# Routing logits as extra columns of two projections, and the choice of experts on raw logits

## What is computed

```python
x = x + retention(layernorm(x) @ Wq, layernorm(x) @ Wk, layernorm(x) @ Wv) @ Wo
# retention, per chunk and head: attn = (q k^T) * D;  o = attn v + (q * decay_q) S
#                                S = decay_s * S + (k * decay_k)^T v
t = layernorm(x)
probs = softmax(t @ Wg)                       # 8 experts
top_w, top_i = top_k(probs, 2); top_w /= sum(top_w) + 1e-8
x = x + sum over the chosen e of top_w[e] * (relu(t @ W1[e]) ** 2 @ W2[e])     # W1: 128x256, W2: 256x128
```

## Time and profile before

| what | value |
|---|---|
| median of 3 runs | 287.58 us (287.05 to 288.04) |
| the profiled execution's own time | 287.56 us |
| its span, first to last instruction | 285.8 us |
| busy share of the span: PE, DVE, POOL, ACT | 95%, 77%, 72%, 64% |
| DMA: moved, mean rate | 26.80 MB, 94 GB/s |
| granted clock of PE | 0.999 |
| one loop pass in the middle | 32.58 us |

### The profile page before, as it was taken

One profiled execution on the slowest core, in us unless ns is written; L12 is line 12 of the kernel. 1 busy time (PEld: TensorE's weight loads), 2 busy tenths in 40 slices (PEclk: granted clock), 3 DMA queues, 4 the chain that ended last, 5 costly groups with the idle time before them and its releaser, 6 DMA issues.

```text
span 285.8 us, 8944 instructions
## 1 busy us (share of the span) xinstructions
PE 272.0 (95%) x3662; PEld 214.0 (75%) x3662; DVE 219.2 (77%) x569; ACT 182.7 (64%) x265; POOL 205.3 (72%) x165
## 2 busy tenths in 40 slices
PE   7979859799999999999999999999999999999995
PEld 6566538568887788777887788777887788878883
DVE  3749848996769965996769965896859768998783
ACT  2354569466873697556964687556965567686861
POOL 2114888878969698669968699579968668566452
PEclk9999999999999999999999999999999999999999
DMA  7429043213250251304450250203420252043201
GB/s 233 128 60 304 7 189 100 84 31 124 76 148 2 78 186 48 103 5 136 126 147 2 79 175 15 71 5 108 153 76 2 77 158 90 17 141 119 76 0 73
DMA packets 13577, 26.80 MB, mean 94 GB/s; under 512 B 1120, under 2 KB 6624, under 8 KB 13536
## 3 DMA queue, kind: packets, MB, share of 16 engines
q1 hardware_dynamic: 13536, 26.23, 28.5%
HBM read 24.00 MB, written 2.23 MB: 92 GB/s over the span
## 4 chain that ended last, share of the span: by engine, by line
PE 56%; POOL 17%; issue 15%; DVE 5%; DMA 2%; ACT 2%; POOLq 1%; DVEq 0%
POOL act_lo L1067 14%; PE h_ps L338 7%; PE y_ps L353 6%; PE h_ps L340 6%; PE h_ps L339 6%; PE y_ps L359 6%; PE y_ps L354 6%; PE bank L485 3%; POOL rstd L1021 2%; PE bank L507 2%; PE bank L418 2%; PE bank L497 2%; DMA scale<-scratch 1%; PE bank L450 1%; PE y_ps L317 1%
## 5 line engine op out<-in xcount | busy, mean ns | idle before, releaser
L1067 POOL TENSOR_TENSOR act_lo<-act_f,act_hi 128x512 fp32r<-128x512 f32 x112 | 145.6, 1324 | 46.0 <-ACT act_f L955 45.9
L765 DVE SCALAR_TENSOR_TENSOR act_s<-h_ps,scale 128x1024 f32<-128x1024 f32 x64 | 77.9, 1218 | 29.6 <-PE h_ps L340 13.5
L950 ACT ACTIVATE act_hi<-act_s 128x1024 fp32r<-128x1024 f32 x64 | 67.8, 1059 | 29.7 <-DVE act_s L765 29.5
L955 ACT ACTIVATE act_f<-act_s 128x1024 f32<-128x1024 f32 x64 | 66.8, 1044 | 0.0
L338 PE MATMUL h_ps<-x_hi,w_lo 128*128 128x512 f32 x128 | 53.9, 421 | 1.7 <-DVE attn L658 1.7
L353 PE MATMUL y_ps<-act_hi,w_lo 128*128 128x512 f32 x128 | 53.8, 421 | 0.0
L340 PE MATMUL h_ps<-x_hi,w_hi 128*128 128x512 f32 x128 | 50.6, 395 | 0.0
L339 PE MATMUL h_ps<-x_lo,w_hi 128*128 128x512 f32 x128 | 50.4, 394 | 0.0
L354 PE MATMUL y_ps<-act_hi,w_hi 128*128 128x512 f32 x128 | 50.2, 392 | 0.0
L359 PE MATMUL y_ps<-act_lo,w_hi 128*128 128x512 f32 x128 | 40.4, 396 | 0.1
L1021 POOL TENSOR_TENSOR rstd<-variance,minus_half 128x4 f32<-128x4 f32 x16 | 18.4, 1152 | 19.5 <-DVE variance L622 19.4
(11 more groups left out here) (123 smaller groups left out, 387.8 us busy)
## 6 DMA issues: line engine op xcount, KB each, us to landing
scale<-scratch SPq DMA_DIRECT2D x32, 512.0 KB, 4.0
x_t_in<-x_tr SPq DMA_DIRECT2D x8, 256.0 KB, 4.9
x_all<-x SPq DMA_DIRECT2D x8, 256.0 KB, 4.8
out<-out_sb SPq DMA_DIRECT2D x8, 256.0 KB, 4.1
scale<-w SPq DMA_DIRECT2D x1, 768.0 KB, 4.7
cst<-constants SPq DMA_DIRECT2D x1, 417.0 KB, 4.8
cst<-constants SPq DMA_DIRECT2D x1, 256.0 KB, 2.8
scale<-w SPq DMA_DIRECT2D x1, 256.0 KB, 5.6
```

Source lines behind the costliest of these rows:

```text
L765: nc.vector.scalar_tensor_tensor(out=act_s[:, u % 2], in0=h_ps[:, u % 2], scalar=0.0, in1=scale[:, f % 2, e].unsqueeze(1).to_broadcast([P, ...
L950: nc.scalar.activation(act_hi[:, u % 4], act_s[:, u % 2], ACT.Square).then_inc(act_hi_ready, 1)
L955: nc.scalar.activation(act_f[:, u % 2], act_s[:, u % 2], ACT.Square).then_inc(act_f_ready, 1)
L1067: nc.gpsimd.tensor_tensor(act_lo[:, u % 4, n], act_f[:, u % 2, n], act_hi[:, u % 4, n].bitcast(F32), ALU.subtract).then_inc(pool_low_ready, 1)
```

## The change

The routing logits no longer have a stage of their own. Since x2 = x + rstd * (o Wo), the raw logits x2 @ (centred Wg) are x @ Wg' + rstd * (o @ (Wo Wg')). The first term comes as 8 more columns of the value projection, the second as 8 more of the output projection, whose weights are made once on the chip (`route_outputs`). ACT's `copy_v` copies the first 8 columns for each group next to x (the rows of x_all are 136 wide now), and `add_attention` adds the second with the same instructions that make x2. The two best are found on these raw logits (`rank_experts`, `mark_chosen`), the shift is applied to the sorted values, now from SBUF (`shift_logits`), ACT makes the eight exponentials and two of half the argument, POOL takes the inverse square root of the denominator only (4 values per partition), and DVE multiplies.

With wider groups four of them no longer fit one PSUM bank: the fourth goes to another bank. `project_out` uses bank2 for it, so `project_q(a)` has to wait for x2 and is split from `project_k(a)`. The orders change: on PE slot 1 k, 3 q, 4 transposes of k, 5 value projection; in the start `transpose_roots(0)` stands ahead of `w1_product(0, 0)` and the outputs; on DVE the key is decayed before the query, and the choice is split; on POOL the lower parts of W1 come after the roots.

```diff
-        x_all = sb("x_all", [P, X_RING, GROUPS, P])
+        x_all = sb("x_all", [P, X_RING, GROUPS, WIDE])
+        def v_place(s, g):
+            if g == GROUPS - 1:
+                return ((y_ps[:], h_bank[3])[s] if s < 2 else bank1[:])[:, 0:WIDE]
+            return ((bank1[:], h_bank[2])[s] if s < 2 else bank2[:])[:, WIDE * g:WIDE * (g + 1)]
+
+        def out_place(g):
+            return bank2[:, 0:WIDE] if g == GROUPS - 1 else bank1[:, WIDE * g:WIDE * (g + 1)]
...
+            def route_outputs():
+                pe.wait_ge(second_loaded, DMA)
+                pe.wait_ge(v_z_ready, 1)
+                pe.matmul(y_ps[:, 0:EXPERTS], cst[:, C_WO_T:C_WO_T + P], w_g, start=True, stop=True).then_inc(wog_done, 1)
...
+            def project_q(s):
...
+                else:
+                    pe.wait_ge(x2_ready, s)
+                project(s, 0, q_bank(s), q_done)
...
             def project_v(s):
...
                     pe.wait_ge(q_m_ready, s + 1)
                     pe.wait_ge(q_d_ready, s + 1)
+                    pe.wait_ge(x_hi_ready, s)
...
-                    last = pe.matmul(v_bank(s)[:, P * g:P * (g + 1)], x_t_in[:, s % XT_RING, P * g:P * (g + 1)],
-                                     w_center[:, 2], start=True, stop=True)
+                    last = pe.matmul(v_place(s, g), x_t_in[:, s % XT_RING, P * g:P * (g + 1)], w_vg, start=True, stop=True)
...
-            def route(s):
-                pe.wait_ge(x_sum_ready, s + 1)
...
                     if n == 1:
-                        project_qk(a)
+                        project_k(a)
                     if n == 3:
+                        project_q(a)
+                    if n == 4:
                         transpose_k(a)
-                    if n == 4:
+                    if n == 5:
                         project_v(a)
...
             center_piece(2)
             center_piece(3)
+            center_piece(4)
+            transpose_roots(0)
             w1_product(0, 0)
-            center_piece(4)
             outputs_within(1, (0, 1))
-            transpose_roots(0)
             w1_product(0, 1)
...
+            def rank_experts(s):
+                raw = x_all[:, s % X_RING, :, P:WIDE]
+                dve.wait_ge(x2_ready, s + 1)
+                for g in range(GROUPS):
+                    last = nc.vector.max(best[:, g], raw[:, g])
+                last.then_inc(rank_step, 1)
...
                 for g in range(GROUPS):
-                    last = nc.vector.tensor_scalar(logits[:, g], l_ps[:, g], top[:, g:g + 1],
+                    last = nc.vector.tensor_scalar(shifted[:, g], best[:, g], best[:, g, 0:1],
                                                    rstd[:, 1, s % STAT_RING, g:g + 1], ALU.subtract, ALU.mult)
...
+            def weigh(s):
...
                 dve.wait_ge(expd_ready, s + 1)
+                nc.vector.tensor_reduce(total[:], expd[:], AX_X, ALU.add).then_inc(weigh_step, 1)
...
+                nc.vector.scalar_tensor_tensor(out=denom[:, 0], in0=total[:], scalar=TOP_EPS, in1=expd[:, :, 0],
+                                               op0=ALU.mult, op1=ALU.add).then_inc(weigh_step, 1)
...
-                if a < TILES:
-                    decay_q(a)
                 scale_h(f, 1)
                 low(u)
                 if a < TILES:
                     decay_k(a)
+                    decay_q(a)
                 scale_h(f, 2)
                 low(u + 1)
                 if p < TILES:
+                    rank_experts(p)
                     shift_logits(p)
                 scale_h(f, 3)
                 low(u + 2)
                 if p < TILES:
-                    choose(p)
+                    mark_chosen(p)
+                    weigh(p)
                 if a < TILES:
                     decay_scores(a, decay_order(a)[0:1])
                 scale_h(f, 4)
                 low(u + 3)
                 if a < TILES:
-                    decay_scores(a, decay_order(a)[1:2])
+                    decay_scores(a, decay_order(a)[1:3])
                 if p < TILES:
                     spread_roots(p)
                 if a < TILES:
-                    decay_scores(a, decay_order(a)[2:])
+                    decay_scores(a, decay_order(a)[3:])
...
                 for g in range(GROUPS):
+                    nc.scalar.copy(x_all[:, s % X_RING, g, P:WIDE], v_place(s, g)[:, P:WIDE])
                     last = nc.scalar.activation(v_z[:, s % 2, PAIRS * g:PAIRS * (g + 1), ::3],
...
-                nc.scalar.activation(expd[:], logits[:], ACT.Exp).then_inc(expd_ready, 1)
+                nc.scalar.activation(expd[:], shifted[:], ACT.Exp)
+                nc.scalar.activation(half_expd[:], shifted[:, :, 0:TOP], ACT.Exp, scale=0.5).then_inc(expd_ready, 1)
...
+                nc.gpsimd.tensor_tensor(r_denom[:], denom[:, 2], minus_half[:], ALU.pow).then_inc(r_denom_ready, 1)
...
+            root_denominators(0)
+            pool.wait_ge(combine_ready, 1)
             low_piece(1)
-            root_shares(0)
-            pool.wait_ge(combine_ready, 1)
             low_piece(2)
```

More of the change, by code:

```diff
@@ L93, in build @@
         minus_half = sb("minus_half", [P, GROUPS])
-        half = sb("half", [P, GROUPS * TOP])
         stats = sb("stats", [P, 2, STAT_RING, GROUPS, 6])
@@ L177, in build @@
         ident = cst[:, C_IDENT:C_IDENT + P]
-        w_out = cst[:, C_WO:C_WO + P]
-        wg_in = cst[:, C_WG:C_WG + EXPERTS]
+        w_out = cst[:, C_WO:C_WO + WIDE]
+        w_q, w_k, w_v = (w_center[:, P * n:P * (n + 1)] for n in range(3))
+        w_vg, w_g = w_center[:, 2 * P:], w_center[:, 3 * P:]
         center_loaded, first_loaded, second_loaded = sem("center_loaded"), sem("first_loaded"), sem("second_loaded")
@@ L395, in project_qk @@
                 if s < 3:
                     pe.wait_ge(x_t_loaded[s % XT_RING], DMA * (s // XT_RING + 1))
-                    pe.matmul(q_bank(s), w_center[:, 0], x_t_in[:, s % XT_RING], start=True, stop=True).then_inc(q_done, 1)
-                    pe.matmul(k_bank(s), w_center[:, 1], x_t_in[:, s % XT_RING], start=True, stop=True).then_inc(k_done, 1)
+                    pe.matmul(place_of, (w_q, w_k)[n], x_t_in[:, s % XT_RING], start=True, stop=True).then_inc(done, 1)
                     return
@@ L402, in project_qk, with project_k @@
                 pe.wait_ge(x_t_low, s - 2)
-                for n, (place_of, done) in enumerate(((q_bank(s), q_done), (k_bank(s), k_done))):
-                    pe.matmul(place_of, w_qk_lo[:, n], x_t_hi[:], start=True, stop=False)
-                    pe.matmul(place_of, w_qk_hi[:, n], x_t_lo[:], start=False, stop=False)
-                    pe.matmul(place_of, w_qk_hi[:, n], x_t_hi[:], start=False, stop=True).then_inc(done, 1)
+                pe.matmul(place_of, w_qk_lo[:, n], x_t_hi[:], start=True, stop=False)
+                pe.matmul(place_of, w_qk_hi[:, n], x_t_lo[:], start=False, stop=False)
+                pe.matmul(place_of, w_qk_hi[:, n], x_t_hi[:], start=False, stop=True).then_inc(done, 1)
+            def project_q(s):
+                if s == 0:
+                    pe.wait_ge(w_center_ready, 1)
+                elif s == 1:
+                    pe.wait_ge(attn_ready, 1)
+                else:
+                    pe.wait_ge(x2_ready, s)
+                project(s, 0, q_bank(s), q_done)
+            def project_k(s):
+                if s == 1:
+                    pe.wait_ge(attn_ready, 2)
+                elif s >= 2:
+                    pe.wait_ge(root_t_ready, s - 1)
+                    pe.wait_ge(attn_ready, PAIRS * s)
+                    if s == 2:
+                        pe.wait_ge(piece_whole, PIECES)
+                project(s, 1, k_bank(s), k_done)
             def project_v(s):
                 if s == 1:
-                    pe.wait_ge(attn_ready, 3)
+                    pe.wait_ge(attn_ready, PAIRS)
                 elif s >= 2:
@@ L714, in choose, with weighed @@
+            def weigh(s):
+                def weighed(n):
+                    dve.wait_ge(weigh_step, WEIGH_STEPS * s + n)
                 dve.wait_ge(expd_ready, s + 1)
-                for g in range(GROUPS):
-                    last = nc.vector.max(best[:, g], expd[:, g])
-                last.then_inc(choose_step, 1)
-                nc.vector.tensor_reduce(total[:], expd[:], AX_X, ALU.add).then_inc(choose_step, 1)
-                chosen_step(1)
-                for g in range(GROUPS):
-                    last = nc.vector.max_index(best_at[:, g], best[:, g], expd[:, g])
@@ L988, in _ @@
                 square(u)
-                if f >= 1 and a < TILES:
-                    mask_q(a)
+                if a < TILES:
                     copy_k(a)
@@ L1090, in _ @@
                     low(u - 1)
+                if f == 0:
+                    root_variance(p, 1)
                 low(u)
+                if 1 <= f and p < TILES:
+                    root_variance(p, 1)
                 if p < TILES:
-                    root_variance(p, 1)
                     low_x(p)
```

231 lines of the change are left out of this document (107 added, 124 removed).

## The result

| | before | after |
|---|---|---|
| median of the runs | 287.33 us (287.05 to 288.04, 4 runs) | 291.56 us (290.90 to 291.62, 4 runs) |
| profiled execution, its span | 287.56, 285.8 | 291.50, 289.7 |
| busy: PE, DVE, POOL, ACT | 272.0, 219.2, 205.3, 182.7 | 271.0, 230.4, 199.0, 185.3 |

The changed kernel is slower by 1.4%: ratio 1.0138, 95% interval 1.0113 to 1.0163. The forecast was 281.1 us, with a range of 279.2 to 285.3. The sign was wrong and the range missed.

The account below looks back on a forecast made before the run. PE, busy 95% of the span, was taken to bound the kernel. Middle 5.28 - 0.33 - 1.0 = 3.95 plus start 2.5 gave 6.45 us less: 281.1 us, with an 8-in-10 range of 279.2 to 285.3.

Parts of the forecast that it names:

- Removed from PE: Middle, after 58.31: six routing slots of 0.88 us each leave PE, 5.28 us saved.
- Columns, 0.03 each: Eight more columns on value and output projections cost PE 0.03 us, eleven times: 0.33 us, bounds 0 and 0.55.
- The wait for q_d, 0.2: Before the value projection PE waits 0.2 us for DVE's scaled query, five times: 1.0 us lost.
- All this lies beside PE at no cost; without the cover ACT's 0.9 would be the price.: Middle tiles: changed work on ACT, DVE and POOL costs PE nothing; ACT's added load is about 0.9 us a tile.
- The rival with late scores: Each middle tile: DVE, held by POOL, delivers decayed scores 0.9 us late at e = 5, five times: 285.6 us; chance 0.24.
- the likeliest case: The forecast itself, whole kernel: 281.1 us, own range 279.0 to 283.6, chance 0.48.
- The start: Up to tile 2's state updates: 2.5 us shorter, from the removed routing slot and vanished score waits; bounds 1 and 3.3.
- The first link: Start: earlier root transposes and a shorter choice bring the weights' broadcast to between 36.6 and 38.2, before the first scaling.
- the place of that wait is taken by the projection: add_attention(1) starts at 38.8: Start: add_attention(1) waits for tile 1's output projection instead of the scaling, starting at 38.8, not 40.83.
- The end: After the last output projection: 0.85 us less, with one removed routing slot of 0.88 counted there.
- The rival "slower": Five tiles: POOL's lock on DVE at its worst makes first decayed scores 2.5 us late each: 293.6 us; chance 0.05.

Follow-up runs that it names:

- the last kernel of 7: Changed kernel with expert-sum copy before values', logit shift on ACT, query decayed before key, old start order on POOL and PE: 283.50 us, ratio 0.9813 to the kernel before.
- the query first: Changed kernel with expert-sum copy before values' and shift on ACT, plus DVE decaying query before key: 284.32 us, ratio 0.9838; also tried with earlier exponentials, 286.04 us.
- 4: Kernel before, with only the value projection and routing slots exchanged, so the value projection comes one slot later: 295.32 us, ratio 1.0223 to the kernel before.
- 1: Changed kernel with ACT copying the finished expert sum (copy_y) ahead of the values (copy_v): 291.38 us, ratio 1.0132 to the kernel before.
- 5: Changed kernel with the start's old order, lower W1 piece earlier on POOL and first W1 product earlier on PE: 290.06 us; POOL's part only: 292.48 us.
- 2: Changed kernel with the logit shift moved from DVE to ACT, maximum not subtracted: 289.16 us, ratio 1.0066 to the kernel before.

## Why the prediction was wrong

Its own steps, in order.

- **Removed from PE**: right. Up to w1(3) the tile is 0.50 shorter after, and 0.75 in the last kernel of 7, which has no wait there: 0.89 less the columns and about 0.1 in products that each take 0.01 to 0.02 longer, for which I have no cause.
- **Columns, 0.03 each**: right. 0.84 against 0.81 for the value projection, 0.83 against 0.81 for the output projection.
- **The wait for q_d, 0.2**: right in size, 0.19 and 0.07 behind it, and shown by the query first, 0.28 a tile.
- **"All this lies beside PE at no cost; without the cover ACT's 0.9 would be the price."** This is the step that failed in the middle. I followed what waits for the value projection on PE and DVE, and took ACT's changes as a load against its idle time. The load was indeed small. But ACT's program is an order, and the sum of the pass before stood behind the values, with 1.49 in hand that the earlier trace rows and ACT's timeline would have shown. The move took 1.68 of it and PE's earlier demand 0.5, so that the reserve of 1.49 became a lack of 0.7. Shown: by the same wait with the move alone (4), and by its absence when the copy goes first (1). Price: 0.84 a tile, 4.2 of the 5.3 missed in five.
- **The rival with late scores**: its mechanism is there, and its instant, 120.85, was right within 0.2; the wait is 0.55 against the 0.9 worked out, for PE asks 0.15 later than it had assumed. But it lies behind the wait for y_t, so that after's profile doesn't show it in a full tile, and the likeliest case and the rival were both incomplete. By the Trainium skill (SBUF — State Buffer, Who interferes with whom) VectorE's tensor_scalar in its two-port mode blocks against GpSimd. This case's trace agrees: 280 ns in the median from PSUM and SBUF alike, and nine of the 32 from SBUF held until POOL's instruction ends. I had put the shift at 0.85 and a wait of 1.15 in the rival and the wait at nothing in the forecast; four took 1.80, and 3.08 at 48.48 in the first pass. The argument against this rival, that such waits rarely fall together, is refuted by the rows, where one shift and both instructions of the weighing are held in each of the five tiles.
- **The start**: sum 2.5, measured -1.1. The first link held: the scale landed for a scaling at 36.44, a little ahead of 36.6 to 38.2. The failed step is "the place of that wait is taken by the projection: add_attention(1) starts at 38.8", which took the projection's own start, 37.58, as given. It was not: the transposes put ahead of `w1_product(0, 0)` hold it, with the low clock behind, and it starts at 39.91, `add_attention(1)` at 41.14. That is 2.3 to 2.4 of the 3.6 missed, and the late decayed scores of the first pass are the other 1.2. Shown by 5: with the order of before for that product 1.8 us come back, and by 2: with the shift taken off DVE the projection starts at 37.52 and the start is 2.7 shorter. Of the 2.4 between 39.91 and 37.52, 1.0 is that the first product starts earlier (30.59, not 31.62) and 1.2 that its six matmuls take 1.50, not 2.69. With all mended the start is 2.9 shorter than before.
- **The end**: counted as another slot of 0.88. It has waits of 0.20 and 0.70 for DVE's scaling and roots in the pass after the last output projection, and came out 0.6 longer. With the shift on ACT they are gone and it is 0.6 shorter than before (53.05 against 53.7), so DVE's lateness is what the forecast left out here too.

The rival "slower" had the right sign for a wrong reason: it put 2.5 us a tile on DVE alone. The true case was two smaller waits, a start that lost, and an end that lost.

What stays open: when the clock falls (POOL's order alone moves the slow stretch, and in some executions of one kernel it is there and in others not); whether PE's order alone would mend the start; and what makes the products 0.01 to 0.02 longer.

## What to carry to other kernels

When a slot of work moves later, walk the program of every engine that consumes it, and list what is queued behind each consumer with its reserve; a busy share of 64% says nothing of an engine that waits in order. When a wait is predicted or removed, look for the next one at the same place: here two of about 0.55 lay side by side, and in the tile each mend alone was worth little. Look at least, median and most of a small instruction, not at its mean: 557 ns were 280 and, in nine of 32, the rest of another engine's instruction. Don't put work that waits ahead of work that is ready on the bounding engine, in a thin start above all, where its idle time can cost it the clock as well.

## What the runs showed of the hardware

- A wait of PE costs more than its idle entry: 0.57 idle, 0.84 in the distance between products; 0.55 idle, 0.81 (2.22 and 1.49 where 1.50 and 1.40 go without a wait).
- A wait can be there without an idle entry: 0.19 before the value projection is only seen as 1.67 between starts.
- After 3.60 us with PE busy for 1.41, the next six matmuls of 512 columns took 0.43 each, not 0.23, with a granted clock of 0.54. The same product at 30.59 and at 28.44 in other kernels ran at full clock; so did the one at 31.41 with POOL's order alone, after the same 1.41 in 3.60, and the slow stretch came later.
- DVE's `tensor_scalar` on 128x8 in float32 takes 277 ns in the median from PSUM and 280 from SBUF. From SBUF, nine of 32 took 1154 to 1432, each until 26 to 30 ns behind the end of a POOL instruction that works in SBUF; from PSUM none of 32 took over 286, eight of them wholly beside POOL's work.
- Instructions of DVE with two operands in SBUF do the same: on 128x4, 0.17 beside an idle POOL, 1.01 and 1.20 beside its remainders, with ends 0.02 to 0.03 behind POOL's.
